# Moving the code passes of a fused transformer layer from SyncE to ScalarE, and three neighbours of them in their queues

## The reference, cut to what matters

```
x = x + cross_attention(layernorm(x), context)      # context: 12544 x 512, 16 heads of 32
x = x + self_attention(layernorm(x))                # 16 heads of 128
x = x + mixture_of_experts(layernorm(x))            # 32 experts, 4 per row, plus a shared one

cross_attention: q = rms_norm(x Wq + bq) * gq
                 text keys   k = rms_norm(c Wk + bk) * gk,  v = c Wv + bv     (12287 rows)
                 image keys  the same with weights of their own               (257 rows)
                 out = (softmax(q k')v over text + softmax(q k')v over image) Wo + bo
self_attention:  w = codes * repeat(scales, 32, axis=0)      # for q, k, v and o
                 q = x wq + bq, ... ; softmax(q k' / sqrt(128)) v ; wo
```

## Time and profile before

| | |
|---|---|
| timed executions | 1199.26, 1200.07, 1204.12 us |
| the profiled execution's own time | 1197.79 us |
| its span, first to last instruction | 1196.1 us |
| TensorE busy | 1154.2 us (96%) |
| VectorE, ScalarE, GpSimd busy | 947.6, 876.7, 764.0 us (79%, 73%, 64%) |
| granted clock of TensorE, mean over the span | 0.99 |
| stretch of steps 2 to 23 | 90.09 to 901.17 us |

### The profile page before, as it was taken

One profiled execution on the slowest core, in us unless ns is written; L12 is line 12 of the kernel. 1 busy time (PEld: TensorE's weight loads), 2 busy tenths in 40 slices (PEclk: granted clock), 3 DMA queues, 4 the chain that ended last, 5 costly groups with the idle time before them and its releaser, 6 DMA issues.

```text
span 1196.1 us, 26329 instructions
## 1 busy us (share of the span) xinstructions
PE 1154.2 (96%) x8794; PEld 950.5 (79%) x8794; DVE 947.6 (79%) x1611; ACT 876.7 (73%) x1891; POOL 764.0 (64%) x1064
## 2 busy tenths in 40 slices
PE   6999999999999999999999999999998879899998
PEld 4778888888888888888888888888887658588886
DVE  4778788887788787787878887778887778499997
ACT  5577877778777777777787777877777757388885
POOL 7988788887889788898887887888873000000000
PEclk9999999999999999999999999999999989899999
DMA  7135677665875657766667665686654899579990
GB/s 257 40 97 153 170 194 184 175 180 158 215 191 152 171 168 204 195 168 175 177 170 195 181 172 167 170 209 166 184 140 108 252 394 398 208 270 362 364 369 15
DMA packets 129327, 236.72 MB, mean 198 GB/s; under 512 B 15014, under 2 KB 42150, under 8 KB 128812
## 3 DMA queue, kind: packets, MB, share of 16 engines
q1 hardware_dynamic: 129196, 235.05, 66.5%
HBM read 140.87 MB, written 17.04 MB: 132 GB/s over the span
## 4 chain that ended last, share of the span: by engine, by line
PE 61%; POOL 11%; SPq 11%; DVE 6%; DMA 4%; issue 4%; ACT 2%; POOLq 0%; DVEq 0%; ACTq 0%
PE ps L1573 22%; PE ps L1437 12%; SPq L354 10%; PE ps L1599 5%; PE ps L1632 4%; DMA code_scale<-code_scales 3%; PE ps L1800 3%; PE ps L1803 3%; PE ps L1806 3%; POOL cx_blocks L624 2%; DVE small L1197 2%; POOL cx_blocks L622 2%; PE ps L1821 1%; PE ps L1829 1%; PE ps L1825 1%
## 5 line engine op out<-in xcount | busy, mean ns | idle before, releaser
L1573 PE MATMUL ps<-w_text,cx_blocks 128*128 128x512 f32 x1974 | 488.2, 394 | 0.5 <-ACT v_first L814 0.5
L1573 PEld LDWEIGHTS ps<-w_text,cx_blocks 128*128 128x128 f32 x1974 | 366.9, 188 | 86.8 <-issue 7.7
L857 ACT ACTIVATE p<-ps,small 128x512 f32<-128x512 f32 (+2 forms) x400 | 272.3, 682 | 116.7 <-DVE small L1199 112.8
L1197 DVE TENSOR_REDUCE small<-ps 128x1 f32<-128x512 f32 (+2 forms) x400 | 269.7, 674 | 87.4 <-PE ps L1599 86.9
L1437 PE MATMUL ps<-ident,p 128*128 128x128 f32 x1584 | 209.0, 273 | 11.0 <-DVE pt L1191 7.0
L1437 PEld LDWEIGHTS ps<-ident,p 128*128 128x128 f32 x1584 | 184.8, 141 | 41.2 <-issue 11.5
L839 ACT ACTIVATE pt<-ps 128x512 f32<-128x512 f32 (+1 forms) x296 | 164.4, 589 | 36.9 <-PE ps L1437 36.8
L622 POOL TENSOR_TENSOR cx_blocks<-cx_sum,small 128x256 fp32r<-128x256 f32 x188 | 119.1, 633 | 82.5 <-PE ps L1573 69.0
L624 POOL TENSOR_TENSOR cx_blocks<-cx_sum,cx_blocks 128x256 fp32r<-128x256 f32 x188 | 140.3, 746 | 14.7
L1599 PE MATMUL ps<-k_stack,q_stack 96*128 96x512 f32 (+1 forms) x400 | 146.2, 438 | 2.0 <-ACT p L857 1.7
L1199 DVE TENSOR_TENSOR small<-small 128x1 f32<-128x1 f32 x400 | 132.6, 331 | 13.7
(11 more groups left out here) (252 smaller groups left out, 1923.3 us busy)
## 6 DMA issues: line engine op xcount, KB each, us to landing
expert<-experts SPq DMA_DIRECT2D x34, 1536.0 KB, 8.7
k_stack<-kt_hi SPq DMA_DIRECT2D x384, 128.0 KB, 3.3
cx<-ctx_t SPq DMA_DIRECT2D x48, 512.0 KB, 5.0
k_stack<-kt_lo SPq DMA_DIRECT2D x192, 128.0 KB, 3.1
codes<-codes SPq DMA_DIRECT2D x64, 256.0 KB, 3.1
code_scale<-code_scales SPq DMA_DIRECT2D x64, 256.0 KB, 3.8
scaled<-codes SPq DMA_DIRECT2D x64, 256.0 KB, 2.3
weight_q<-scaled SPq DMA_DIRECT2D x1, 4096.0 KB, 15.3
```

The source lines that it names most:

```text
L857: eng.activation(pb[:, lo:hi], score_bank(s, h)[:, lo:hi], exp, bias=nm[1 - par][:, h:h + 1], accum_out=ls[1 - par][:, h:h + 1]).then_inc( ...
L1197: eng.tensor_reduce(ngm[:, h:h + 1], score_bank(s, h)[:, lo:hi], AX.X, ALU.max, negate=True).then_inc(e_gm, 1)
L1573: last = eng.matmul(ps_a[(p + i + 1) % 2][:, :], blk[:, i, a, c * P:(c + 1) * P], w_t[:, i, w, c * D:(c + 1) * D], start=(i in FRESH and c ...
```

## The change

1. **Code passes.** `pass_codes` leaves SyncE's queue and enters ScalarE's. The three passes stand at the ends of ScalarE's slots `j` 1, 4 and 7, in each step the same three passes as before. Their waits and their DMAs are the same.
2. **Code scalings on GpSimd.** The first of a step goes from before `third_sum(0)` to behind `split(0, 4)`; the second from before `split_first(1)` to behind `key_norm(s + 1, 0)`; the third from before `split(1, 3)` to behind `split(1, 6)`, the end of the step.
3. **The last key norm.** `first_sums` is cut into `first_sum` and `second_sum`, and for the second pair `key_norm(s, 3)` goes between them, one sum earlier.
4. **The rescaling.** `scale_attention` is cut into `scale_sums` (L1212, L1215), now at the end of VectorE's `j == 1`, and `scale_attention` (L1225), now at the end of `j == 2`. In the last steps, which are written otherwise (`drain`), both stay where they were.

```diff
# SyncE
-            def pass_codes(s, k, m, loop):
-            ...
                 if nxt and (loop or s > 0):
                     eng.wait_ge(e_ab, s * (2 * NPOS))
                     load(s + 1, 1)
-                if s > 0:
-                    pass_codes(s - 1, 2, (s - 1) % UNROLL, loop)
-                pass_codes(s, 0, m, loop)
...
-                pass_codes(s, 1, m, loop)
                 if 1 <= s < NG:
                     load_next(s)
# GpSimd
                 if strass:
                     split(0, 2, sum_y[:, :, :], 2)
                     split(0, 3, sum_x[:, :, :], 0)
+                    third_sum(0)
+                    split(0, 4, sum_x[:, :, :], 3)
                 scale_codes(s * W_STEP - (W_FIRST * W_STEP + 1), (m + 1) % 2, loop)
                 if strass:
-                    third_sum(0)
-                    split(0, 4, sum_x[:, :, :], 3)
                     fourth_sum(0)
...
                 if nxt:
-                    first_sums(1)
+                    first_sum(1)
                 if cur:
                     key_norm(s, 3, 1)
+                if nxt:
+                    second_sum(1)
                 if strass:
                     split(0, 6, quarter(0, 1, 1), 0)
-                scale_codes(s * W_STEP - W_FIRST * W_STEP, m % 2, loop)
                 if nxt:
                     split_first(1)
                     if s > 0:
                         key_norm(s + 1, 0, 1)
...
+                scale_codes(s * W_STEP - W_FIRST * W_STEP, m % 2, loop)
+                if nxt:
                     split(1, 2, sum_y[:, :, :], 2)
-                scale_codes(s * W_STEP - (W_FIRST * W_STEP - 1), (m + 1) % 2, loop)
-                if nxt:
                     split(1, 3, sum_x[:, :, :], 0)
...
                     split(1, 6, quarter(1, 1, 1), 0)
+                scale_codes(s * W_STEP - (W_FIRST * W_STEP - 1), (m + 1) % 2, loop)
# ScalarE, at the end of slot(j)
+                    if j == 1:
+                        pass_codes(s - 1, 2, (s - 1) % UNROLL, loop)
+                    if j == 4:
+                        pass_codes(s, 0, m, loop)
+                    if j == 7:
+                        pass_codes(s, 1, m, loop)
# VectorE, in slot(j) and drain(h)
-                    if end and j == 5:
+                    if end and s < NG - 1 and j == 1:
+                        scale_sums()
+                    if end and s < NG - 1 and j == 2:
                         scale_attention()
...
                     if end and h == 12:
+                        scale_sums()
                         scale_attention()
```

More of the change, by code:

```diff
@@ L586, in free, with first_sum @@
                         eng.wait_ge(e_pp, s * (2 * NPOS) + (NPOS * (p - 1) + i + 1))
-                def first_sums(p):
+                def first_sum(p):
                     eng.wait_ge(e_c[p], s * 16 + 16)
@@ L593, in first_sums, with second_sum @@
                     eng.tensor_tensor(sum_x[:, :, :], quarter(p, 0, 1), quarter(p, 1, 1), ALU.add).then_inc(e_sum, 1)
+                def second_sum(p):
                     eng.wait_ge(e_sum, s * 8 + (4 * p - 3))
@@ L629, in step @@
                 if strass:
-                    first_sums(0)
+                    first_sum(0)
+                    second_sum(0)
                 if cur:
@@ L814, in plain_values, with pass_codes @@
                 eng.activation(v_first[1][j][:, :], ps_a[0][:, :], copy).then_inc(e_v, 1)
+            def pass_codes(s, k, m, loop):
+                i = s * W_STEP + (k - W_FIRST * W_STEP)
+                if not loop and not 0 <= i <= NW:
+                    return
+                b = (m + k) % 2
+                if loop or i >= 1:
+                    eng.wait_ge(e_cm, i)
+                    eng.dma_start(tile_of(scaled, i - 1).rearrange("o p f -> p (o f)"), codes[1 - b][:, :]).then_inc(e_cs[1 - b], 16)
+                if not loop and i == NW:
+                    return
+                if loop or i >= 2:
+                    eng.wait_ge(e_cs[b], i * 8 - 8 * b)
+                eng.dma_start(codes[b][:, :], tile_of(t["codes"], i).rearrange("o p f -> p (o f)")).then_inc(e_cl[b], 16)
+                eng.dma_start(code_scale[:, :], tile_of(t["code_scales"], i).rearrange("o p f -> p (o f)")).then_inc(e_cl[b], 16)
             def step(eng, s, m, loop=False):
@@ L1204, in maximum, with scale_sums @@
                         eng.tensor_tensor(dm, nm[1 - par], old, ALU.subtract).then_inc(e_dm, 1)
-                def scale_attention():
+                def scale_sums():
                     eng.wait_ge(e_al, (s - 2) + 1)
@@ L1215, in scale_attention @@
                     eng.tensor_tensor(l_st[st], l_st[st], ls[par], ALU.add).then_inc(e_l2, 1)
+                def scale_attention():
                     o3 = by_head(o_st[st])
```

## The result

The changed kernel takes 1225.58 us (1223.25 to 1227.66, four runs) against 1199.66 of the kernel before beside it: 2.1% slower, ratio 1.0208, 95% interval 1.0176 to 1.0240. 1191 had been forecast. The profiled execution took 1226.41 us, with a span of 1224.6; that is 28.5 more than the span before.

The account below looks back on a forecast made before the run. TensorE's own work was taken as the bound, with 11.7 us of stalls to win (6.8 key tiles, 4.1 exponentials, 0.9 stack DMAs). Profiled 1197.79 - 11.7 + 2.7 for late steps = 1188.8, plus 2.28 = 1191 us median; range 1187 to 1208.

Parts of the forecast that it names:

- B: Pass of j 7 slowed to 3.1 us by SyncE's stack(1) issues; TensorE waits in j 1; 1214 to 1221 us; chance 0.16.
- The bound and the gain: TensorE's own work bounds steps 2 to 23; 36.87 us each against 36.34 without stall, so 11.7 us can be won.
- The third scaling: End of GpSimd's step: scales asked for in j 7 return in time for key tile 1's norm, 0.8 us to spare.
- the ring: ScalarE's j 7 request, landing, GpSimd's scaling, sums and norm, ScalarE's use at key tile 1: 8.3 of 9.1 us.
- point of decision: Rival B's threshold: it decides from where the pass of j 7 takes over 2.5 us.
- What is queued behind the waits: Behind ScalarE's passes, free time before TensorE is delayed: 0.82 us at j 4, 1.3 at j 1, 1.9 at j 7.
- Passes on ScalarE: Issuing a pass on ScalarE takes 0.7 us, 1.30 less 0.6 overlapped; it fits the free time at j 1, 4, 7.
- Last norm and first scaling: On GpSimd, norm sooner and first scaling later remove TensorE's waits for key tiles: 6.8 us gained.
- Rescaling: On VectorE, moved into idle time before j 2 and j 3, it removes TensorE's exponential waits: 4.1 us gained, no cost.
- SyncE's queue: Nine DMAs per step leave SyncE, 3.9 us of issuing; 0.9 us of stack waits go, nothing else is bound there.
- Rival A: Issuing is serial: ScalarE stands 1.30 us a pass, j 4 costs 0.48 a step, 11 us, so 1199.5; chance 0.23.
- C: Code transfers collide with those of stack(1), delaying ScalarE's high keys up to 1 us: 11 us, so 1199; chance 0.08.

Follow-up runs that it names:

- the two opened versions: Changed kernel, third pass at end of j 6, last-row loads behind stack(1) of step 24; with third scaling behind next step's key_norm(s, 2) 1191.48 us, without 1192.29.
- Experiments 1 and 5: Changed kernel, third scaling behind next step's key_norm(s, 2): 1196.54 us; plus third pass at j 6 and later last-row loads: 1191.48; those two alone: 1192.29.
- experiment 7: Kernel before, passes on SyncE, with rescaling 1203.25 us; norm, rescaling 1197.88; first scaling 1194.57; norm, first scaling 1195.44; all three 1189.67.
- experiment 3: Changed kernel with each pass's two loads issued ahead of its store, scales first: 1204.45 us, ratio 1.0039.
- experiment 6: Changed kernel with the code passes back in SyncE's queue, parts 2 to 4 left: 1253.97 us, ratio 1.0434.

## Why the prediction was wrong

The forecast and its chances pointed the wrong way; the rival with the right sign, B, had 0.16.

- *The bound and the gain.* Right. The floor of 36.34 us and the 11.7 us above it stood; the two opened versions are 9.4 and 10.2 us faster than the kernel before, by the medians.
- *The third scaling: the step that failed.* The sum gave the ring 9.1 us and charged 8.3, "3.8 to landing". It took 6.3 on the median of the j 7 passes, so the same sum is 10.8, 1.7 more than the 9.1. In the step shown it took 7.2, the sum is 11.7, and ScalarE's wait should be 2.6; it was 3.54. Of the 0.9 between, 0.7 is the lead, which was 8.4 us and not 9.1 (468.48 to 476.91, when ScalarE asked). The rest of the sum holds well: by it a landing of up to 3.8 + 0.8 = 4.6 us is free, and the steps with 4.2 to 4.8 are the ones without a loss. I took the median of 64 landings for a DMA that the change puts into the middle of twelve others. The trace of before held a warning: its first pass of a step, behind a stack and a context load, landed its scales after 4.6 us on the median and up to 5.4, which leaves nothing of the 0.8. Range and rivals should have carried a landing beside a stack.
- *Rival B.* Its ring was the right one. Its price, 26 to 33 us, stands above the floor, where the measured steps are 22 x (38.00 - 36.34) = 36.5, and its 1214 to 1221 fell short of 1225.58. Its cause was not the one: ScalarE's issues in j 7 of step 11 took 0.35, 0.66 and 0.77 us, 1.84 for the pass and not 3.1. What its point of decision named, the pass's own time, never came near 2.5 there (1.33 to 1.91 over the steps). And it named j 1 for the stall; it is j 2.
- *What is queued behind the waits.* For the pass of j 1 I named copies and exponentials, and took the exponential of head 5, with 1.3 us free, for the tightest. It was the copy of the partial product, first in the queue, that TensorE needs sooner.
- *Passes on ScalarE.* The price, 0.7 us with nothing of it on the path, was right in what counts. In the timeline above the first issue starts at 468.48, 0.01 after the exponential two operations ahead of it in the program began; the engine then stands 1.17; over the 22 steps it stands 43.4 us for issuing, 0.66 a pass. Experiments 1 and 5 show that none of it need reach TensorE.
- *Last norm and first scaling.* The gain of 6.8 was granted to both; the scaling's place brings 5 us alone, and the norm adds nothing to that (experiment 7). In the changed kernel neither could act, as GpSimd was late from the ring.
- *Rescaling.* "4.1 gained, no cost" was right on the waits at the scores and wrong on the time: alone, it gains nothing (1203.25 us), and with the first scaling later 5.8 us. In the one trace of it alone the waits come back at the key tiles.
- *SyncE's queue.* "Nothing else is bound there" missed step 24. The wait for the last store stayed on SyncE while the store moved behind ScalarE's j 7; about 2.5 of the 5.4 us are this wait, and 3.1 are longer busy time at the lower granted clock, which no term had.
- *Rival A* and *C*: neither as written. ScalarE's waits for `k_stack` rose from 3.6 to 7.7 us, 4.1 of it in step 24 alone. The transfers did meet, as C has it, but it is the scales that land late beside the stack, and not the stack.

The rule from the Trainium skill that B was set beside (Perfetto Trace Analysis, DMA Instruction — HWDGE: one generator, locked for one sequencer, the lock wait part of the issue) agrees in sign: the scales' issue took 0.73 us on the median of the j 7 passes, among SyncE's stack issues of 0.60 to 0.83, and 0.48 on that of the j 4 passes. No run here tells a lock from a full queue.

Left open: how the landing doubles beside a stack. The transfers of the pass and of twelve stack DMAs then run together, with the DMA engines busy all the time (1.05), and experiment 3 shows that being first in the pass brings it down to 3.4 us; but no run took the stack away. Open is also what draws the falls of the granted clock in step 24 and in experiment 6: the ones looked at came with idle time of TensorE, but idle time of the same length elsewhere brought none. The chip time of one execution also moves by several us from run to run in most versions, and each of them has waits that some steps have and some don't; what draws them was not tried.

## What to carry to other kernels

Before a DMA is moved, price its landing by rows with the same neighbours in flight, not by the median of where it is now. When a load's request and its use stand in two engines' lists, write the whole ring down (request, landing, use, what is behind the use, who asks for that) and compare it with the time that the loop gives; here it decided whether a turn was free (landing of 4.8 us or less) or cost 0.5 to 4 us. And a wait removed at one slot of a loop that several engines keep just in step is only gained once the next late engine is early.

## What the runs showed of the hardware

- ScalarE's queue issues a DMA while its engine is still busy with operations that stand ahead of it in the program: the pass of j 7 began its first issue 0.01 us after the start of the last exponential, before that one's accumulator read.
- Loads of 256 KB issued third on ScalarE's queue landed after 3.0 us (median) where SyncE's queue was quiet and after 6.3 us (4.2 to 8.3) where twelve DMAs of 128 KB were being issued on it. Issued first instead of third, they landed after 2.6 and 3.4 us.
- The granted clock of TensorE fell to 1.2 GHz for 3.4 us at a time, 14 times in the 22 steps of the version with many short waits (experiment 6, mean 0.97), never in those of the kernel before (1.00).
